# Two message-passing layers: one ring for gathered rows and sums, gathers in other numbers and at other moments

## The reference

```python
# x: 100000 x 256 fp32; src, dst: 25000 node numbers, sorted by dst; edge_weight: 25000
deg = maximum(segment_sum(ones, dst, 100000), 1.0);  s = deg ** -0.5
h = maximum(layernorm(x), 0.0)
x = x + s * segment_sum((s * h)[dst] * edge_weight, src)          # layer 0
h = maximum(layernorm(x), 0.0)                                      # layer 1
feat = concat([h[dst], h[src] - h[dst]])                            # 25000 x 512
msg = relu(feat @ W1 + b1) @ W2 + b2                                # 512 -> 512 -> 256
x = x + segment_sum(msg, dst) / (count(dst) + 1e-8)
```

## Time and profile before

| | us |
|---|---|
| median of 3 executions | 2254.42 |
| lowest, highest | 2254.40, 2258.35 |
| the profiled execution, its own time | 2253.34 |
| its span, first to last instruction | 2251.5 |
| busy in it: PE | 1767.0 |
| busy in it: DVE | 1496.5 |
| busy in it: POOL | 1280.7 |
| busy in it: ACT | 1034.8 |

### The profile page before, as it was taken

How to read it: one execution, slowest core, us unless ns; L and a number is a source line. 1 busy time by engine, 2 the same in 40 slices (tenths; PEclk the granted TensorE clock), 3 DMA queues, 4 the chain that set the end, 5 groups by cost and what they waited for, 6 DMA issues and landing times.

```text
span 2251.5 us, 46578 instructions
## 1 busy us (share of the span) xinstructions
PE 1767.0 (78%) x14020; PEld 1537.2 (68%) x14020; DVE 1496.5 (66%) x6002; ACT 1034.8 (46%) x2106; POOL 1280.7 (57%) x1024
## 2 busy tenths in 40 slices
PE   7958787886666667303888888889999999989995
PEld 2258777786566667303776776778888888878875
DVE  8969888996666667303555555567777776757573
ACT  0024444453333333203454554556666775656563
POOL 2033332478888788655222222246888888888874
PEclk9989999998878888656998888899999999999998
DMA  8989999566555656457898999623555555545553
GB/s 295 317 294 326 321 338 310 148 112 103 103 102 105 103 101 107 56 106 223 300 297 284 300 300 289 205 70 71 95 95 92 95 96 91 96 90 97 89 89 38
DMA packets 142804, 379.84 MB, mean 169 GB/s; under 512 B 31806, under 2 KB 97353, under 8 KB 129865
## 3 DMA queue, kind: packets, MB, share of 16 engines
q0 software_dynamic: 86400, 131.14, 32.4%
q1 hardware_dynamic: 27452, 208.63, 27.1%
q10 hardware_dynamic: 28912, 39.64, 6.6%
HBM read 325.72 MB, written 259.17 MB: 260 GB/s over the span
## 4 chain that ended last, share of the span: by engine, by line
POOL 16%; PE 15%; issue 13%; another core or an unknown queue 4%; ACT 3%; DVE 3%; DMA 1%; ACTq 1%; DVEq 0%; POOLq 0%
PE ps_h L1224 9%; POOL table_out L932 9%; POOL ends L920 7%; PE ps_m L1238 2%; PE ps_s L1251 2%; DVE e_moments L974 1%; PE ps_t L1211 1%; ACT feat_hi L1130 1%; ACT hid L1137 1%; ACT ends L1123 1%; DVE out_sum L1046 1%; DVE feat_lo L1041 1%; DMA table_out<-e_ring,e_targets_all 1%; ACT e_ring L1155 0%
## 5 line engine op out<-in xcount | busy, mean ns | idle before, releaser
L920 POOL DMA_INDIRECT ends<-x,keys x400 | 399.8, 1000 | 436.2 <-PE ps_t L1211 312.3
L772 PE MATMUL ps_deg<-table,hot 128*128 128x128 bf16 x5600 | 357.9, 225 | 75.6 <-issue 66.8
L1224 PE MATMUL ps_h<-feat_hi,w_hi 128*128 128x512 f32 x800 | 337.1, 421 | 94.2 <-ACT hid L1137 77.8
L772 PEld LDWEIGHTS ps_deg<-table,hot 128*128 128x128 bf16 x5600 | 334.7, 101 | 94.1 <-issue 82.6
L465 POOL DMA_INDIRECT x<-sums_ring,targets_all x200 | 329.2, 1646 | 88.8 <-issue 65.0
L932 POOL DMA_INDIRECT table_out<-e_ring,e_targets_all x200 | 328.6, 1643 | 86.3 <-issue 58.7
L455 POOL DMA_INDIRECT rows<-in_x,row_idx x200 | 208.7, 1043 | 243.9 <-ACT normed L699 190.1
L1224 PE MATMUL ps_h<-feat_lo,w_hi 128*128 128x512 f32 x800 | 330.4, 413 | 0.0
L1224 PE MATMUL ps_h<-feat_hi,w_lo 128*128 128x512 f32 x800 | 329.2, 412 | 0.0
L786 PE MATMUL ps_sum<-msg_hi,same 128*128 128x260 f32 x800 | 154.9, 324 | 155.3 <-issue 148.9
L1224 PEld LDWEIGHTS ps_h<-feat_hi,w_hi 128*128 128x128 f32 x800 | 159.8, 200 | 147.8 <-ACT hid L1137 89.2
(11 more groups left out here) (141 smaller groups left out, 3538.6 us busy)
## 6 DMA issues: line engine op xcount, KB each, us to landing
table_out<-x SPq DMA_DIRECT2D x400, 252.0 KB
x<-in_x SPq DMA_DIRECT2D x400, 250.0 KB
hi_row<-hi_rows ACTq DMA_DIRECT2D x50, 256.0 KB
src_row<-src_rows ACTq DMA_DIRECT2D x50, 256.0 KB
dst_row<-dst_rows ACTq DMA_DIRECT2D x50, 256.0 KB
ends<-x,keys POOLq DMA_INDIRECT x400
rows<-in_x,row_idx POOLq DMA_INDIRECT x200
x<-sums_ring,targets_all POOLq DMA_INDIRECT x200
```

What stands on the lines that cost most here:

```text
L772: last = nc.tensor.matmul(ps_deg[q][k][:, j * P:(j + 1) * P], hot[:, c, k, j * P:(j + 1) * P], table[:, c, part, :], start=(c == 0 and par ...
L920: pool.indirect_dma_start(out=ends[b % NE][:, n, :], out_offset=None, in_=x1_d, in_offset=bass.IndirectOffsetOnAxis(ap=keys[:, 1 - end, at ...
L1224: last = nc.tensor.matmul(ps_h[m % 2][:], w[:, k, m * P:(m + 1) * P], f[:, k, :], start=(k == 0 and n == 0), stop=(k == KF - 1 and n == 2))
```

## The change

**Layer 0.** One ring `slots` of 30 places holds first a batch's gathered rows, then, in place, its normalized rows, and in the end its sums. `rows`, `normed`, `sums_ring` and the semaphore `ring_free` go. The lead is 28 batches; each gather of a batch b of 7 and more waits until batch b - 7 has its variance (`var_done`); and after the four gathers of a batch POOL waits until they have landed and tells VectorE (`rows_ready`). In the loop there are two gathers per iteration instead of 5/2.

**Layer 1.** The lead is 20 batches instead of 22. In the lead, every pair of gathers first waits in the new function `pace` for a point of the step three batches back. In the loop there are 11/4 gathers per group instead of 5/2.

```diff
-    RING0 = 26
+    SLOTS = 30
-    LEAD0 = 24
-    LEAD1 = 22
+    LEAD0 = 28
+    AHEAD0 = 7
+    LEAD1 = 20
...
-            sums_ring = sb("sums_ring", [P, RING0, W, CW], fp32)
+            slots = sb("slots", [P, SLOTS, W, CW], fp32)
...
                 def gather(b, j):
-                    if j == 0 and b >= 2:
-                        pool.wait_ge(normed_done, b + 1)
                     pool.indirect_dma_start(
-                        out=rows[b % 2][:, j, :], out_offset=None, in_=x,
+                        out=slots[:, b % SLOTS, j, 0:D], out_offset=None, in_=x,
...
-                        .then_inc(rows_in[b % 2], 16)
+                        .then_inc(rows_in[b % 4], 16)
+                def gathered(b):
+                    pool.wait_ge(rows_in[b % 4], 16 * W * (b // 4 + 1))
+                    pool.sem_inc(rows_ready, 1)
...
                 def scatter_end(b):
                     pool.wait_ge(scattered, 16 * W * (b + 1))
-                    pool.sem_inc(ring_free, 1)
                 for b in range(LEAD0):
+                    if b >= AHEAD0:
+                        pool.wait_ge(var_done, b - AHEAD0 + 1)
                     for j in range(W):
                         gather(b, j)
+                    gathered(b)
...
                 left = W * (NB - LEAD0)
+                ready = LEAD0
                 for b in range(NB):
+                    first, last = min(left, 2 * b // 1), min(left, 2 * (b + 1) // 1)
                     scatter(b)
-                    for n in range(min(left, 5 * b // 2), min(left, 5 * (b + 1) // 2)):
+                    while ready < LEAD0 + first // W:
+                        gathered(ready)
+                        ready += 1
+                    for n in range(first, last):
                         gather(LEAD0 + n // W, n % W)
                     scatter_end(b)
...
                 def moments_of(b, t, q):
-                    dve.wait_ge(rows_in[q], 16 * W * (t + 1))
+                    dve.wait_ge(rows_ready, b + 1)
+                    dve.sem_inc(waited, 1)
                     for j in range(W):
-                        last = nc.vector.bn_stats(moments[:, j, :], rows[q][:, j, :])
+                        last = nc.vector.bn_stats(moments[:, j, :], slots[:, bass.ds(b % SLOTS, 1), j, 0:D]
+                                                  .rearrange("p o d -> p (o d)"))
...
                 def norm(b, t, q):
                     act.wait_ge(shift_done, b + 1)
+                    act.sem_inc(waited, 1)
                     for j in range(W):
-                        last = nc.scalar.activation(normed[q][:, j, :], rows[q][:, j, :], ACT.Relu,
+                        row = slots[:, bass.ds(b % SLOTS, 1), j, 0:D]
+                        last = nc.scalar.activation(row, row, ACT.Relu,
                                                     bias=shift[q][:, j:j + 1], scale=rstd[q][:, j:j + 1])
...
                 def to_ring(b, t, q):
                     act.wait_ge(summed, b + 2)
-                    act.wait_ge(ring_free, b + 1)
...
+                def pace(b, n):
+                    if b == 1 and n == 0:
+                        pool.wait_ge(ends_in[0], 16 * 2 * W)
+                    elif b == 2:
+                        if n == 0:
+                            pool.wait_ge(ends_in[1], 16 * 2 * W)
+                        elif n < 6:
+                            pool.wait_ge(turned, n)
+                        else:
+                            pool.wait_ge(mm1_done, 1)
+                    elif b >= 3:
+                        if n < 4:
+                            pool.wait_ge(mm1_done, KH * (b - 3) + 2 + n)
+                        else:
+                            pool.wait_ge(mm2_done, GROUPS * (b - 3) + n // 2 - 1)
                 for b in range(LEAD1):
                     for n in range(2 * W):
+                        if n % 2 == 0:
+                            pace(b, n)
                         gather(b, n)
...
-                    for n in range(min(left, 5 * c // 2), min(left, 5 * (c + 1) // 2)):
+                    for n in range(min(left, 11 * c // 4), min(left, 11 * (c + 1) // 4)):
                         gather(LEAD1 + n // (2 * W), n % (2 * W))
```

More of the change, by code:

```diff
@@ L364, in pb @@
                 return stage.enter_context(nc.psum_tensor(name, shape, dt))
-            rows = [sb(f"rows{q}", [P, W, D], fp32) for q in range(2)]
             src_row = [sb(f"src_row{q}", [P, W * P], fp32) for q in range(2)]
@@ L374, in gnn_preln_two_layers @@
             shift = [sb(f"shift{q}", [P, W], fp32) for q in range(2)]
-            normed = [sb(f"normed{q}", [P, W, D], fp32) for q in range(2)]
             hot = sb("hot", [P, C, 2, W * P], bf16)
@@ L400, in gnn_preln_two_layers @@
             ps_sum = [pb(f"ps_sum{a}", [P, 512], fp32) for a in range(W)]
-            rows_in = [sem(f"rows_in{q}") for q in range(2)]
+            rows_in = [sem(f"rows_in{u}") for u in range(4)]
+            rows_ready = sem("rows_ready")
             src_row_in = [sem(f"src_row_in{q}") for q in range(2)]
@@ L425, in gnn_preln_two_layers @@
             in_ring = sem("in_ring")
-            ring_free = sem("ring_free")
             idx_steps = sem("idx_steps")
@@ L448, in _ @@
                     nc.gpsimd.memset(msg_hi[:, j, D + j:D + j + 1].bitcast(fp32), 1.0).then_inc(cnt_cols, 1)
-                pool.sem_inc(ring_free, RING0)
                 def gather(b, j):
-                    if j == 0 and b >= 2:
-                        pool.wait_ge(normed_done, b + 1)
                     pool.indirect_dma_start(
-                        out=rows[b % 2][:, j, :], out_offset=None, in_=x,
+                        out=slots[:, b % SLOTS, j, 0:D], out_offset=None, in_=x,
                         in_offset=bass.IndirectOffsetOnAxis(ap=row_idx[:, W * b + j:W * b + j + 1], axis=0))\
-                        .then_inc(rows_in[b % 2], 16)
+                        .then_inc(rows_in[b % 4], 16)
+                def gathered(b):
+                    pool.wait_ge(rows_in[b % 4], 16 * W * (b // 4 + 1))
+                    pool.sem_inc(rows_ready, 1)
                 def scatter(b):
@@ L466, in scatter @@
                             out=x1_d, out_offset=bass.IndirectOffsetOnAxis(ap=targets_all[:, b, j:j + 1], axis=0),
-                            in_=sums_ring[:, b % RING0, j, 0:D], in_offset=None, compute_op=ALU.add)\
+                            in_=slots[:, b % SLOTS, j, 0:D], in_offset=None, compute_op=ALU.add)\
                             .then_inc(scattered, 16)
@@ L583, in dup_tiles_of @@
                     dve.wait_ge(in_ring, b + 1)
-                    nc.vector.tensor_tensor(dup_tile[:], sums_ring[:, bass.ds(b % RING0, 1), :, D:CW]
+                    nc.vector.tensor_tensor(dup_tile[:], slots[:, bass.ds(b % SLOTS, 1), :, D:CW]
                                             .rearrange("p o j c -> p (o j) c"), later_tile[:], ALU.mult)\
@@ L711, in message @@
                     act.wait_ge(summed, b + 1)
+                    act.sem_inc(waited, 1)
                     for j in range(W):
-                        last = nc.scalar.activation(msg[:, j, :], normed[q][:, j, :], ACT.Copy,
+                        last = nc.scalar.activation(msg[:, j, :], slots[:, bass.ds(b % SLOTS, 1), j, 0:D], ACT.Copy,
                                                     scale=coef[q][:, j:j + 1])
@@ L720, in to_ring @@
                     act.wait_ge(summed, b + 2)
-                    act.wait_ge(ring_free, b + 1)
                     act.sem_inc(waited, 1)
                     for j in range(W):
-                        last = nc.scalar.activation(sums_ring[:, bass.ds(b % RING0, 1), j, :], ps_sum[j][:, 0:CW],
+                        last = nc.scalar.activation(slots[:, bass.ds(b % SLOTS, 1), j, :], ps_sum[j][:, 0:CW],
                                                     ACT.Copy)
```

## The result

The changed kernel takes 2149.07 us (median of 4 executions, 2142.3 to 2150.86), the kernel before beside it 2254.41 us (2253.12 to 2258.35): a ratio of 0.952, 95% interval 0.9502 to 0.9538. The profiled execution took 2147.31 us, its span is 2145.5 us, 106.0 us less than before. This was measured on one chip. On two of the four chips of the experiments the kernel before itself took only 2132 to 2134 us; the changed kernel was not run there.

The account below looks back on a forecast made before the run. POOL's calendar was taken to bound the kernel, a lead and a loop of additions per layer: 1 - 18 - 72 + 14 = -75 us against 2253.34 us, forecast 2178 us, range 2146 to 2240 us.

Parts of the forecast that it names:

- the step: Layer 1's lead under the copy: a step near 21.5 us instead of 27.5, 20.7 if all holes go.
- the clock: Layer 1 under the copy: TensorE's clock near 1.0 instead of 0.88, named as a sign of being right.
- the missing holes: Layer 1's lead: no hole ahead of bias addition out_sum, which had waited 7.95 us without a named releaser.
- Layer 0's lead: Gathers ahead of layer 0's additions: the additions start about as before, +1 us (-13 to +24).
- c: Layer 0's lead under the copy: time from a batch's first gather issue to its landing, taken as 11.5 us.
- the rival of the throttled lead: Layer 0's lead is throttled by landings of 13 to 16 us per batch: total 2201 to 2234 us; chance 0.13.
- Layer 0's loop: Layer 0's additions: 88 gathers left instead of 104, 533.6 us against 551.6, so -18 us (-44 to -10).
- Layer 1's lead: Gathers ahead of layer 1's additions: pairs shorten the step, additions start at 1445 instead of 1516.67 us, -72 us (-79 to -3).
- The limit is then the copy: Layer 1's lead: up to 23.3 us per step, additions start when the copy ends, 1445 us (1438 to 1452).
- Layer 1's loop: Layer 1's additions: 240 gathers instead of 224, 2.75 per group, 737.4 us against 723.6, so +14 us.
- pairs help partly or not: Layer 1's lead: the copy makes the holes; total 2244 us without relief, 2199 with half; chance 0.21.
- Handovers come late while many gathers are queued: Layer 1's lead: the reading of holes that end with the bursts; pairs keep the queue short, step near 21.5 us.

Follow-up runs that it names:

- experiment 3: The changed kernel without the waits of pace in layer 1's lead, so bursts of eight gathers, on chip A: 2237.8 us.
- experiment 6: The changed kernel with layer 1's lead in bursts of 8, waiting only where a batch's first pair waits: 2142.51 us on chip B, 2216.81 us on chip C.
- experiment 5: The changed kernel with layer 1's lead paced in fours instead of pairs: 2151.09 us on chip B; 2149.16 us on chip D, 1.0078 of the kernel before.

## Why the prediction was right, and where its numbers came from elsewhere

The forecast was 2178 us; 2149.07 is inside the range and 29 us below. The mechanism was right, two terms were mis-sized in opposite directions, and that the result lies inside the range is in part luck: with layer 1's lead as measured and all else as predicted the working gives 2253.34 + 1 - 18 - 122.65 + 14 = 2127.7 us, below the range. Of the signs named ahead, the step, the clock and the missing holes came; the first addition at 435 us (461.97), layer 1's first gather at 984 (1007.59) and its first addition 444 us later (392.7) did not, and landings of 10 us under a copy, named as a sign of being wrong, did occur in layer 0.

- **Layer 0's lead: +1 predicted, +28 measured** (461.97 - 434.00). The mis-sized term is c, taken as 11.5 us between bounds of 8.4 and 13.0. It was 13.36. The one row that measured it directly in layer 0 (13.0) was right. The earlier trace rows was read rightly too, for the same batch of the changed kernel waits 3.66 us, but it does not carry over: the batch ahead of it waits 8.85 us, and layer 0's 6 to 12. At c = 13.0 the same working gives 458. It is the rival of the throttled lead, at the edge of its 13 to 16; it did not show in the total because layer 1 gave more. The Trainium skill's fit (DMA: Bandwidth & Descriptors, Anatomy of one DMA) gives an estimate of 2.3 us for such a gather. The 2.63 us of waiting behind the copy are near it; under the copy it fails, with 6 to 12 us.
- **Layer 0's loop: -18 predicted, -21.5 measured** (530.1 against 551.6), with 10.95 us per iteration as predicted. The five without gathers became shorter, 9.71 instead of 10.35 us, which is most of the difference. Lead and loop together: layer 1 starts 6.3 us later than before, not 17 sooner.
- **Layer 1's lead: -72 predicted, -122.65 measured.** The step came down as argued, to 20.5 us (21.5 predicted), and the holes ahead of out_sum vanished. The step that failed is the next one: "The limit is then the copy", with the copy's end kept at 1445 us. I had seen the DMA engines at 0.90 and 294 GB/s, and took it for the copy's own speed. But the copy is slow where there are holes (295 to 297 GB/s in the kernel before, in experiment 3, and in experiment 6 on chip C) and faster where there are none. I put that down to the same stalls, since SyncE issues each piece and its instruction stream stood still as well; no run separates the two. In the changed kernel it moves at 332 GB/s and ends near 1398 us. 515.3 - 392.7 = 123 us, where the fixed end allowed 72.
- **Ahead of the first addition** I expected POOL to wait for the copy. It waits 1.48 us for a product and then 3.78 us more; with layer 0 as before the profile names the copy. Both are within 4 us.
- **Layer 1's loop: +14 predicted, +10.4 measured to the end of the span**; iterations with three gathers took 7.86 us, with two 6.61.
- **The rival "pairs help partly or not"** is refused where the comparison was made: 2237.8 without pairs, 2149.07 with them. The Trainium skill (DMA: Bandwidth & Descriptors, Queues, rings and completion order) has each DMA engine take turns between the rings it has work for, a packet at a time. Chip B's trace does not contradict it: there a burst of 8 leaves the copy at 335 GB/s. What a burst disturbs on chips A and C are instruction streams, of which a rule on packets says nothing, so 2244 us did not follow from it.
- **"Handovers come late while many gathers are queued"** was a reading of one chip's trace. It holds on A and C and not on B and D. Where nothing stalls, the kernel before is at 2132.53 us. Taking its layer 0 and its loop from the first trace, its layer 1 lead there would be 2132.5 - 1.8 - 1001.3 - 734.8 = 394.6 us: as long as the changed kernel's 392.7, set by the copy. The changed kernel itself was not run on such a chip. Fours, its nearest kin, had on chip D layer 1's first gather at 1008.49 (+7), the lead at 393.0 (-2) and 747.4 us from there to the end (+13): +18 us worked out, 16.6 measured. So on such a chip I would expect the change to cost about 0.7%; that is worked out, not measured.

What stays open: why chips differ, whether a chip keeps its kind (no chip showed both: 28 executions of the kernel before at 2244.9 to 2268.6 us, four at 2131.9 to 2133.8; but each chip was seen in one stretch of runs only, and that something other than the chip made the difference is not excluded), and how short a run of gathers must be on a chip with stalls, since fours were never run on one. Whether a copy is needed for the stalls was not tried there either; the shorter hole behind the copy in the earlier trace rows speaks against it.

## What to carry to other kernels

Where idle time has no named releaser, ask of every engine that issues instructions in that moment whether it is late too, the copy's own issuer first: a transfer at 0.90 of the DMA engines is then not at its limit, and removing the stall moves its end as well. Where a trace shows such stalls, space indirect gathers in pairs rather than in bursts, but measure on more than one chip before the cost of it (a lead tied to a product, more gathers in the loop) is accepted. A landing has to be measured under the traffic that it will meet, and a wait for it did better a batch behind the issue (2132.66 against 2149.07 us).

## What the runs showed of the hardware that was not expected

- Chips A and C, and the chip of the result, stall while gathers are issued, most in runs, and B and D do not: SyncE's register moves from 1060 to 1340 us, 29 ns in the median on all, reach 836 to 1512 ns on the one kind and at most 66 on the other, and the kernel before takes 2254 to 2261 or 2133 us.
- In layer 0's lead a batch of four gathers of 128 rows of 1 KB lands 6 to 12 us behind its last issue while the copy runs at 321 GB/s, and 2.6 us behind it once the copy is over. This does not depend on the kind of chip: the lead took 13.7 us per batch on B and 13.2 on C. At layer 1's start the landings under the copy spread from 3.66 to 8.85 us in the changed kernel, and from 6.5 to 9.9 in experiment 5 on chip D.
- Thirty-six gathers within 55 us on chip A went with statistics of the third batch 28 us later (189.31 against 161.08), behind a matmul that was late without a named reason.
